# Attention in a four-layer decoder: own values as one rounded product per unit

## The reference, cut to what matters

```
B, S, HID, D, HQ, HK = 64, 32, 512, 128, 32, 8        # cache: 16 pages x 32 keys = 512
q, k, v = x @ Wq.T, x @ Wk.T, x @ Wv.T                # per head of 128
q, k = rope(rmsnorm(q)), rope(rmsnorm(k))
k_all = concat([cache_k (512), k (32)]);  v_all = concat([cache_v (512), v (32)])
scores = q . k_all / sqrt(128), masked where the cache is not valid
o = softmax(scores) @ v_all                           # f32
x = x + o @ Wo.T;  then three more layers of low-rank adapters
```

## Time and profile before

| | |
|---|---|
| runs | 2484.83 us (median of 3, 2483.62 to 2489.36) |
| the profiled execution | 2491.42 us |
| its span, first to last instruction | 2489.6 us |
| TensorE matmuls | busy 2452.9 us, 99% |
| weight loads | 2144.4 us, 86% |
| VectorE | 1591.1 us, 64% |
| ScalarE | 1233.9 us, 50% |
| GpSimd | 768.0 us, 31% |
| mean granted TensorE clock | 0.996 of full |

### The profile page before, as it was taken

One profiled execution on the slowest core, in us unless ns is written; L12 is line 12 of the kernel. 1 busy time (PEld: TensorE's weight loads), 2 busy tenths in 40 slices (PEclk: granted clock), 3 DMA queues, 4 the chain that ended last, 5 costly groups with the idle time before them and its releaser, 6 DMA issues.

```text
span 2489.6 us, 48454 instructions
## 1 busy us (share of the span) xinstructions
PE 2452.9 (99%) x14960; PEld 2144.4 (86%) x14960; DVE 1591.1 (64%) x4346; ACT 1233.9 (50%) x3084; POOL 768.0 (31%) x854
## 2 busy tenths in 40 slices
PE   8999999999999999999999999999999899999998
PEld 6877777778899999999999999999999788888886
DVE  5777777774577777777777777777776434343333
ACT  4677777775455555555555555555555322222221
POOL 5666666665123332222222211112221211110111
PEclk9999999999999999999999999999999999999999
DMA  5233323335898888888888888888887333333331
GB/s 210 72 102 102 99 88 102 95 92 176 309 321 272 283 276 280 274 273 280 273 278 273 283 275 278 277 275 276 277 275 245 103 104 98 107 97 94 103 97 52
DMA packets 390752, 488.57 MB, mean 196 GB/s; under 512 B 53536, under 2 KB 325152, under 8 KB 387616
## 3 DMA queue, kind: packets, MB, share of 16 engines
q1 hardware_dynamic: 353696, 351.89, 45.1%
q0 software_dynamic: 36864, 134.23, 16.4%
HBM read 397.89 MB, written 88.08 MB: 195 GB/s over the span
## 4 chain that ended last, share of the span: by engine, by line
PE 76%; POOL 10%; issue 7%; ACT 4%; DVE 2%; SPq 1%; DMA 0%; POOLq 0%; ACTq 0%; DVEq 0%
PE s_bank L1014 19%; PE o_bank L1028 18%; POOL q_t L498 7%; PE o_bank L1041 5%; PE pt_a L1054 4%; PE pt_b L1054 4%; PE proj L1502 4%; PE proj L1504 4%; PE proj L1503 4%; ACT normed L562 3%; POOL w_hi L458 2%; POOL w_lo L460 1%; PE acc L728 1%; PE acc L729 1%; PE acc L730 1%
## 5 line engine op out<-in xcount | busy, mean ns | idle before, releaser
L929 ACT ACTIVATE probs<-probs,neg_max 128x544 f32<-128x544 f32 x512 | 383.3, 749 | 556.7 <-DVE neg_max L980 556.7
L980 DVE CUSTOM_DVE_ANT_0 probs<-s_bank,mask 128x544 f32<-128x544 f32 x512 | 371.2, 725 | 311.5 <-PE s_bank L1014 246.9
L1028 PEld LDWEIGHTS o_bank<-p_t,v_c 128*128 128x128 f32 x4096 | 537.4, 192 | 26.2
L1014 PE MATMUL s_bank<-k_t,q_t 128*128 128x288 f32 (+1 forms) x2048 | 556.2, 394 | 2.4 <-DVE neg_max L980 2.4
L1028 PE MATMUL o_bank<-p_t,v_c 128*128 128x128 f32 x4096 | 539.6, 275 | 0.0
L1014 PEld LDWEIGHTS s_bank<-k_t,q_t 128*128 128x128 f32 x2048 | 349.8, 191 | 58.5 <-DVE neg_max L980 4.4
L138 POOL DMA_INDIRECT v_c<-in_v_rows,v_row x256 | 249.1, 973 | 299.1 <-PE o_bank L1028 258.2
L728 PE MATMUL acc<-w_hi,x_hi 128*128 128x512 f32 x764 | 314.9, 412 | 0.0
L498 POOL TENSOR_TENSOR q_t<-normed,v_c 128x256 f32<-128x256 f32 x320 | 248.8, 799 | 182.3 <-ACT normed L562 180.4
L729 PE MATMUL acc<-w_lo,x_hi 128*128 128x512 f32 x764 | 301.4, 394 | 0.0
L730 PE MATMUL acc<-w_hi,x_lo 128*128 128x512 f32 x764 | 300.2, 393 | 0.0
(11 more groups left out here) (157 smaller groups left out, 3962.3 us busy)
## 6 DMA issues: line engine op xcount, KB each, us to landing
k_t<-in_k_pages SPq DMA_DIRECT2D x1024, 128.0 KB
q_spill<-wo_early SPq DMA_DIRECT2D x32, 1024.0 KB, 5.3
q_t<-q_spill SPq DMA_DIRECT2D x64, 512.0 KB
o_spill<-o_t SPq DMA_DIRECT2D x64, 512.0 KB
raw<-o_spill SPq DMA_DIRECT2D x64, 512.0 KB, 3.5
k_t<-in_w_qkv SPq DMA_DIRECT2D x11, 1024.0 KB, 8.1
v_spill<-wo_early SPq DMA_DIRECT2D x8, 1024.0 KB, 7.6
k_spill<-wo_early SPq DMA_DIRECT2D x8, 1024.0 KB, 5.2
```

The source lines that it names most:

```text
L929: nc.scalar.activation(probs[:, j % SLOTS_P], probs[:, j % SLOTS_P], ACT.Exp, scale=-1.0, bias=neg_max[:, j % 2:j % 2 + 1], accum_out=row_ ...
L980: nc.vector.tensor_tensor_reduce(out=probs[:, j % SLOTS_P], in0=s_run, in1=mask[:, par], scale=-SCALE, scalar=3.0e38, op0=ALU.add, op1=ALU ...
L1014: last = pe.matmul(s_bank[:, columns].rearrange("p (s t) -> p s t", t=PSIZE), q_t[:, par, g], k_t[:, par, slots, g], start=True, stop=True)
L1028: last = pe.matmul(o_of(n), v_c[:, par, c, g * HD:(g + 1) * HD], p_t[:, i, c], start=n % QUAD == 0 and c == 0, stop=False)
```

## The change

The own values and the own weights are each split into an upper half, rounded to fp32r, and a lower half, the rounded rest. The four 32-row blocks of one 128-row operand then hold for one unit, on the side of the values: upper, upper, lower, zeros; on the side of the weights: upper, lower, upper, zeros. A single fp32r matmul sums upper x upper, upper x lower and lower x upper. It is done for each unit, right after its cache values, in place of four f32 matmuls per quad; and the own weights are transposed for each unit, where they were once per quad.

ScalarE writes the upper values (two copies of 32x1024, once per batch, at unit 5 of the batch before; for batch 0 at unit 2) and evicts the transposed own weights on its own, 128 columns per unit. VectorE writes the lower values (one subtraction of 32x1024, once per batch, behind the work of unit 6, or of unit 2 for batch 0) and one more small subtraction per unit. SP loads the own values as one transfer per batch, one batch further ahead. GpSimd clears only the rows that hold zeros.

```
+    FIRST_VALUES, VALUES_AT = 2, 5
-        v_own = sb("v_own", [P, 2, HK * HD])
+        v_raw = sb("v_raw", [S, 2, HK * HD])
+        v_own = sb("v_own", [P, 2, HK * HD], F32R)
-        own = sb("own", [P, 2, QUAD, S])
+        own = sb("own", [P, SLOTS_P, QUAD, S], F32R)
-        p_t = sb("p_t", [P, 2, KC + 1, ROWS])
+        p_t = sb("p_t", [P, 2, KC, ROWS])
+        own_t = sb("own_t", [P, 2, ROWS], F32R)
...
# SP
             def load_v_own(b, par):
-                at_least(sp, own_summed, (b - 1) * QUADS)
-                for a in range(QUAD):
-                    to = v_own[a * S:(a + 1) * S, par].rearrange("p (q a d) -> p q a d", a=QUAD, d=HD)[:, :, a]
-                    src = v_dram[bass.ds(b * S, S), :].rearrange("s (q a d) -> s q a d", a=QUAD, d=HD)[:, :, a]
-                    sp.dma_start(to, src).then_inc(v_own_in[par], 16)
+                sp.dma_start(v_raw[:, par], v_dram[bass.ds(b * S, S), :]).then_inc(v_raw_in[par], 16)
...
-                    load_v_own(b, par)
-                    if early:
+                    if early and b == 0:
+                        load_v_own(b, par)
+                    if not (early and b == B - 1):
+                        at_least(sp, v_lo_done, b)
+                        load_v_own(b + 1, 1 - par)
+                    if first:
...
-            sp.wait_ge(own_cleared, 2)
+            sp.wait_ge(projected, NSL * NT)
# GpSimd
-            for par in range(2):
-                nc.gpsimd.memset(v_own[:, par], 0.0).then_inc(own_cleared, 1)
+            nc.gpsimd.memset(v_own[3 * S:4 * S, :, :].bitcast(F32), 0.0).then_inc(own_cleared, 1)
+            pool.wait_ge(own_cleared, 1)
+            nc.gpsimd.memset(own[:, :, 3].bitcast(F32), 0.0).then_inc(own_cleared, 1)
# ScalarE, pt_evacuate
-                upto = KC + 1 if is_last(n) else KC
-                if is_last(n):
-                    at_least(act, own_summed, n // QUAD)
-                nc.scalar.activation(p_t[:, i, LOW:upto]..., pt_b[i][:, 0:(upto - LOW) * ROWS],
+                nc.scalar.activation(p_t[:, i, LOW:KC]..., pt_b[i][:, 0:(KC - LOW) * ROWS],
                                      ACT.Copy).then_inc(pt_b_out, 1)
+                at_least(act, own_summed, n - 1)
+                nc.scalar.activation(own_t[:, i], pt_b[i][:, (KC - LOW) * ROWS:(KC - LOW + 1) * ROWS], ACT.Copy)\
+                    .then_inc(own_out, 1)
+
+            def upper_values(b):
+                act.wait_ge(v_raw_in[b % 2], 16 * (b // 2 + 1))
+                at_least(act, own_summed, (b - 1) * HK)
+                if b < 2:
+                    act.wait_ge(projected, NSL * NT)
+                for k in range(2):
+                    nc.scalar.activation(v_own[k * S:(k + 1) * S, b % 2], v_raw[:, b % 2], ACT.Copy).then_inc(v_hi_done, 1)
...
                     n = p * UNITS + j
+                    if n == FIRST_VALUES:
+                        upper_values(0)
+                    if n % HK == VALUES_AT and n // HK + 1 < B:
+                        upper_values(n // HK + 1)
                     if n >= LAG:
                         pt_evacuate(n - LAG, (n - LAG) % 2)
# VectorE
-            def normalise(j):
+            def normalise(n, j):
                 inverse = inv_sum[:, j % 2:j % 2 + 1]
-                nc.vector.tensor_scalar(own[:, j // QUAD % 2, j % QUAD], probs[:, j % SLOTS_P, L:KEYS], inverse, None, ALU.mult)\
+                i, of_own = j % SLOTS_P, probs[:, j % SLOTS_P, L:KEYS]
+                nc.vector.tensor_scalar(own[:, i, 0:3:2], of_own.unsqueeze(1).broadcast_to([P, 2, S]), inverse, None, ALU.mult)\
+                    .then_inc(own_hi_done, 1)
+                nc.vector.tensor_scalar(probs[:, i, 0:L], probs[:, i, 0:L], inverse, None, ALU.mult).then_inc(normed, 1)
+                dve.wait_ge(own_hi_done, n + 1)
+                nc.vector.scalar_tensor_tensor(own[:, i, 1], of_own, inverse, own[:, i, 0].bitcast(F32), ALU.mult, ALU.subtract)\
                     .then_inc(normed, 1)
...
+            def lower_values(b):
+                dve.wait_ge(v_hi_done, 2 * b + 2)
+                nc.vector.tensor_tensor(v_own[2 * S:3 * S, b % 2], v_raw[:, b % 2], v_own[0:S, b % 2].bitcast(F32), ALU.subtract)\
+                    .then_inc(v_lo_done, 1)
...
+                        normalise(n - 1, (j - 1) % UNITS)
+                    if n == FIRST_VALUES:
+                        lower_values(0)
+                    if n % HK == VALUES_AT + 1 and n // HK + 1 < B:
+                        lower_values(n // HK + 1)
# TensorE
+            def weigh_own(n):
+                b, g = n // HK, n % HK
+                if g == 0:
+                    pe.wait_ge(v_hi_done, 2 * b + 2)
+                    pe.wait_ge(v_lo_done, b + 1)
+                pe.wait_ge(own_out, n + 1)
+                pe.matmul(o_of(n), v_own[:, b % 2, g * HD:(g + 1) * HD], own_t[:, n % 2], start=False, stop=is_last(n))\
+                    .then_inc(own_summed, 1)
...
             def turn(n):
+                at_least(pe, own_out, n - 1)
                 if n == 0:
                     pe.wait_ge(copied, NV * NT)
+                    pe.wait_ge(own_cleared, 2)
...
-                if is_last(n):
-                    at = KC - LOW
-                    last = pe.transpose(pt_b[i][:, at * ROWS:(at + 1) * ROWS], own_of(n), ident[:, :])
-                last.then_inc(turned, 1)
+                at = KC - LOW
+                pe.transpose(pt_b[i][:, at * ROWS:(at + 1) * ROWS], own_of(n), ident[:, :]).then_inc(turned, 1)
...
                         weigh_values(n - LAG - 1)
-                        if is_last(n - LAG - 1):
-                            weigh_own((n - LAG - 1) // QUAD)
+                        weigh_own(n - LAG - 1)
```

More of the change, by code:

```diff
@@ L792, in own_of @@
         def own_of(n):
-            return own[:, n // QUAD % 2].rearrange("p u s -> p (u s)")
+            return own[:, n % SLOTS_P].rearrange("p k s -> p (k s)").bitcast(F32)
         def is_last(n):
@@ L801, in attend @@
         load_keys, load_queries, name_values, gather_values = loads
-        v_own_in = [sem("v_own_in0"), sem("v_own_in1")]
+        v_raw_in = [sem("v_raw_in0"), sem("v_raw_in1")]
+        v_hi_done, v_lo_done = sem("v_hi_done"), sem("v_lo_done")
+        own_hi_done, own_out = sem("own_hi_done"), sem("own_weights_out")
         own_cleared = sem("own_cleared")
@@ L843, in emit @@
                     early = isinstance(b, int)
+                    first = early and b < len(WO_WITH)
                     if not (early and b < 2):
@@ L856, in _ @@
                 sp.wait_ge(stored[i], 16 * NSL * (NT // QUARTER) // 2)
-            sp.wait_ge(own_cleared, 2)
+            sp.wait_ge(projected, NSL * NT)
             emit(0)
             emit(1)
-            with sp.Fori(2, PAIRS) as p:
+            with sp.Fori(2, PAIRS - 1) as p:
                 emit(p)
+            emit(PAIRS - 1)
             sp.wait_ge(scored, (B - 1) * HK)
@@ L906, in pt_evacuate @@
                 at_least(act, summed, n - 1)
[L907 to L910 removed]
+                nc.scalar.activation(p_t[:, i, LOW:KC].rearrange("p c n -> p (c n)"), pt_b[i][:, 0:(KC - LOW) * ROWS],
                                      ACT.Copy).then_inc(pt_b_out, 1)
+                at_least(act, own_summed, n - 1)
[8 more added lines that the diff above has]
+                    nc.scalar.activation(v_own[k * S:(k + 1) * S, b % 2], v_raw[:, b % 2], ACT.Copy).then_inc(v_hi_done, 1)
             def o_evacuate(quad):
                 b, q = quad // QUADS, quad % QUADS
[L915 removed]
+                act.wait_ge(own_summed, (quad + 1) * QUAD)
                 if q == 0:
@@ L1033, in o_of @@
                 return o_banks[n // QUAD % 2][:, at:at + ROWS]
-            def weigh_own(quad):
-                par = quad // QUADS % 2
-                if quad % QUADS == 0:
-                    pe.wait_ge(v_own_in[par], 16 * QUAD * (quad // (2 * QUADS) + 1))
-                for n in range(quad * QUAD, quad * QUAD + QUAD):
-                    g = n % HK
-                    last = pe.matmul(o_of(n), v_own[:, par, g * HD:(g + 1) * HD], p_t[:, 1, KC], start=False, stop=is_last(n))
-                last.then_inc(own_summed, 1)
+            def weigh_own(n):
[6 more added lines that the diff above has]
+                    .then_inc(own_summed, 1)
             def turn(n):
@@ L1053, in turn @@
                     bank, at = (pt_a, c) if c < LOW else (pt_b, c - LOW)
-                    last = pe.transpose(bank[i][:, at * ROWS:(at + 1) * ROWS],
-                                        probs[:, n % SLOTS_P, c * P:(c + 1) * P], ident[:, :])
-                if is_last(n):
-                    at = KC - LOW
-                    last = pe.transpose(pt_b[i][:, at * ROWS:(at + 1) * ROWS], own_of(n), ident[:, :])
-                last.then_inc(turned, 1)
+                    pe.transpose(bank[i][:, at * ROWS:(at + 1) * ROWS], probs[:, n % SLOTS_P, c * P:(c + 1) * P], ident[:, :])
+                at = KC - LOW
```

(13 more changed lines are left out.)

9 lines of the change are left out of this document (2 added, 7 removed).

## The result

The changed kernel takes **2520.26 us** (median of four runs, 2519.55 to 2522.99), the kernel before beside it on the same chip 2487.10 (2483.62 to 2491.41). The ratio is 1.0135, with a 95% interval of 1.0115 to 1.0154: slower by 1.4%. The forecast was 2473 with a range of 2452 to 2500, so both its sign and its range were wrong.

A forecast was written before the change was run, and what follows sets the result against it. TensorE's streaming was taken to bound attention. Own block -41, lower-values stall +19 and start +10 sum to -12 us, from the median 2484.83 to about 2473 us; own range 2458 to 2486, wider range with rivals 2452 to 2500.

The forecast's parts named there:

- the own block's gain: TensorE, per quad: four f32 products go, three transposes and four rounded products come; -0.32 us, -41 us over 128 quads.
- the second rival: TensorE's own product: rounded at 128 columns no faster than f32, 0.22 us each; 2536 us in all; chance 0.18.
- the load-bound rival: TensorE's own product: a weight load sets its pace, 0.11 us each; 2493 us in all; chance 0.13.
- The stall: TensorE's score waits once per batch for VectorE's masked maximum of unit 7, behind the lower-values subtraction; 0.30 us, +19 us.
- cheap lower half: VectorE's lower-values subtraction: cheap with 32 partitions or hidden by unseen slack, so no stall; 2454 us; chance 0.12.
- ScalarE is hidden: ScalarE's extra eviction per unit and two copies per batch fit into its waits, with 0.8 us to spare; no cost.
- The start: Batch 0: copies wait for the own values' load, delaying unit 2's exponential and unit 3's maximum; +10 us, between 6 and 12.
- The product, 0.06: TensorE's rounded own product of 128 columns costs 0.06 us; range 0.05 to 0.08.
- a sign of being wrong: Listed under what would show the forecast wrong: transposes starting 0.1 or 0.2 us behind the own product.
- The lower values, 0.30: VectorE's 32x1024 subtraction behind unit 6 delays the next score to 2.72 us in a 2.42 step; 0.30 us in 63 batches.
- The range of the term, 8 to 29: Range in us for all stalls behind the lower-values subtraction, around the forecast +19.
- GpSimd, not in the sum at all: GpSimd (POOL) was only said to clear a smaller part, put at nothing; its overlap with VectorE was forecast at 0.

The follow-up runs named there:

- experiment 1: Changed kernel, but from batch 2 on the lower own values are subtracted for only 32 of 1024 columns (output not the reference's): 2477.56 us, 0.9957 of the kernel before.
- Experiment 5: Kernel before plus one unused 32x1024 VectorE subtraction per batch: behind unit 6 2504.34 us (1.0071), behind unit 4 2532.48 us (1.0182).

## Why the prediction was wrong

**What held.** TensorE sets the time and the own block's gain is real: without the stall a step is 2.444 us, and the product is faster than 0.22 (the second rival), with 0.09 between the forecast's 0.06 and the 0.11 of the load-bound rival. The stall is where it was put, in all batches that split values for the next one, with the masked maximum as its releaser, and it isn't hidden: the "cheap lower half" fell, since 32 partitions took 1.217 us as 128 do (1.224), and experiment 1 gave the stall back. ScalarE is hidden in the steady part. The start is right in its mechanism, the order ScalarE, exponential, VectorE, and near in size:

```profile
643.02 5.95 SPq L834 DMA_DIRECT2D v_raw<-v_spill  x3
...
645.25 2.13 ACT L927 ACTIVATE v_own<-v_raw 32x1024 fp32r<-32x1024 f32 x2 [4.71 <-DMA v_raw<-v_spill]
647.41 0.75 ACT L949 ACTIVATE probs<-probs,neg_max 128x544 f32<-128x544 f32 x1
...
648.66 0.72 DVE L1008 CUSTOM_DVE_ANT_0 probs<-s_bank,mask 128x544 f32<-128x544 f32 x1
```

The exponential of unit 2 stands behind the copies (645.25 to 647.41), and the maximum of unit 3 at 648.66, for 650.5 forecast: SP issued the load at 643.02 rather than 644.8, and ScalarE began 2.2 us later, where 2.6 were taken for the landing. The granted clock was 0.75 from 640 to 646 us, 0.82 to 652 and 0.92 to 660, so it came back more slowly than the 0.72 over 6 us of before, as was forecast.

**The product, 0.06.** It measured 0.09, which with the step 0.027 longer is 512 x 0.027 = 14 us of the gain. The step that failed: the pair's weight load was taken as paced by the transpose load behind it, and that one as "shorter by 0.05, some 0.06" because its record is. The spacing of transposes in the kernel before didn't bear this out:

```profile
1212.93 0.38 PE L1054 MATMUL pt_b<-ident,probs 128*128 128x128 f32 x2
```

The two of `pt_a` at 1212.71 have such loads behind them, and the next pair comes 0.22 later, 0.11 for each. In the changed kernel the next transpose starts 0.15 behind the own product, which the prediction itself had named as a sign of being wrong (0.1 or 0.2). The cost lies between the two terms that it weighed, 0.06 and 0.11. This is a size, not a mechanism. By itself it would have left 2487, still in the range of 2452 to 2500 and near no change.

**The lower values, 0.30.** They measured 0.56. The step of the prediction that failed: "Less 0.09 that two operations overlap, it holds the queue for 1.13", from a place "0.70" in the step. The subtraction took 1218.88 - 1217.63 = 1.25 from start to start, and from the small subtraction (1217.36) to it there are 0.27, where 0.15 was taken from the old scaling pair. It let neither the operation ahead nor the one behind overlap, in any of the kernels here. Why is not shown. It isn't that it has two inputs in SBUF; the large subtraction of the last stage, with two such inputs, is overlapped by the next operation, here in the kernel before:

```profile
1947.75 1.21 DVE L191 TENSOR_TENSOR o_lo<-raw,o_hi 128x1024 fp32r<-128x1024 f32 x1
1948.88 0.22 DVE L1408 TENSOR_SCALAR lang_bias<-expert,lang_f 128x8 f32<-128x8 f32 x1
```

That is 1.13 from start to start, the very number of the prediction. What sets the subtraction of the own values apart is its rows: it reads rows 0 to 31 and writes rows 64 to 95, and its neighbours all begin at row 0. It does so in each kernel here that has it, so no run tells whether that is the cause. The maximum stood 0.22 later than thought, the wait from maximum to score was 0.95 and not 0.89, and with the step 0.02 longer the sum is 0.30 + 0.22 + 0.06 - 0.02 = 0.56. The term is a difference of two near-equal numbers, 2.72 and 2.42; an error of 0.1 in either of its parts is a third of it. The range of the term, 8 to 29, was built from other durations of the subtraction only, and the lost overlap with its neighbours, 0.24, wasn't among them.

**GpSimd, not in the sum at all.** It cost 16 us, more than half of the loss of 29. The step that failed is the assumption that VectorE's durations are constant over the 64 batches. The trace of before showed otherwise, in rows that no group of the front has. VectorE's scalings beside GpSimd's split:

```profile
830.39 0.92 DVE L961 TENSOR_SCALAR probs<-probs,inv_sum 128x512 f32<-128x512 f32 x1
...
831.02 0.76 POOL L883 CAST hi_early<-wo_early 128x512 fp32r<-128x512 f32 x1
...
831.85 1.27 POOL L885 TENSOR_TENSOR lo_early<-wo_early,hi_early 128x512 fp32r<-128x512 f32 x1
...
832.49 0.68 DVE L959 TENSOR_SCALAR own<-probs,inv_sum 128x32 f32<-128x32 f32 x1
```

And by the earlier trace rows's view in two narrower stretches: VectorE's busy time was 230.09 us for 737 instructions from 700 to 1000 and 218.81 for the same 737 from 1600 to 1900. That is 11.3 us for the 13 splits that fall into the first stretch (751 to 991 us), 0.87 each, as the two rows above give (0.92 - 0.48 + 0.68 - 0.24 = 0.88), and it cost nothing while VectorE had slack. The sum asked what VectorE adds, and compared it with the slack of an undisturbed step. Asked for the batch with the least slack, the same working gives 0.87 more there, 20 x 0.87 = 17 us, near the 16 measured. The Trainium skill has the mechanism (SBUF — State Buffer, section "SBUF: two separate sides"): VectorE and GpSimd share a pair of SBUF ports as an exclusive lock held for a whole instruction; on VectorE's side it is taken in the modes that use two ports, and by operations with two SBUF inputs against a GpSimd instruction that reads SBUF. The direction agrees: 0.48 to 0.91, 0.24 to 0.59, and GpSimd's subtraction 1.27 to 2.34 beside VectorE's of 1.22. The sizes agree in part: 1.27 + 1.22 would be 2.49, and the scaling of 842.66 ends at 843.57, within GpSimd's conversion (843.26 to 844.03) and not behind it; the first mask build (634.97 to 636.89) does end behind GpSimd's memset (634.81 to 636.61). No run here separates the lock from another cause of the same overlap.

**What would have shown it.** The answer lay in the step lengths. Before the change the distances from one maximum to the next are 2.22, 2.36, 2.25 and 3.14 in the first quad of a batch; the slack in which once-per-batch work can hide is that of the long step, not the mean of 0.5 per step. Experiment 5 is this argument run: in the old kernel the same operation is free behind unit 6, outside the twenty batches, and costs 0.60 in each batch, some 38 us, behind unit 4. Evening out TensorE's steps is a gain for TensorE and takes away the holes of the others at the same time.

## What to carry to other kernels

Before an operation is put on an engine that releases the bottleneck through a single buffer, write down that engine's slack for each step of the period, in the worst period (with every neighbour that stretches its operations), and put the new operation where the longest step is, or cut it into pieces that each fit. A gain that comes from making the bottleneck's steps equal has to be charged with the work of other engines that the long step used to hide. A stall that is the difference of two near-equal sums deserves a range as wide as the errors of all its parts; the cut into four, the choice of units for the pieces and the later first values were together worth more here (53 us) than the whole shorter step (28); a move by one unit alone was worth nothing, and the cut alone 19.

## What was not expected of the hardware

- A VectorE subtraction of 32x1024 takes 1217 ns, one of 128x1024 1224; one of 32x256 takes 417. Fewer partitions bring nothing, fewer elements in the row do: (1217 - 417) / 768 = 1.04 ns each, and some 0.15 us fixed.
- The subtraction that reads rows 0 to 31 and writes rows 64 to 95 doesn't overlap its neighbours on VectorE: 1.25 us from start to start at a duration of 1.22, where a 128x1024 one of 1.21 is followed after 1.13 and the 128x512 scaling of 0.48 after 0.39. The cause is open.
- A second rounded product of 128 columns costs 0.11 us, what a transpose of 128 columns costs too, and the one in its place 0.09. Its 512-column sibling's 0.24 divided by four isn't its price.
- VectorE and GpSimd beside each other: the scalings 0.48 to 0.91 and 0.24 to 0.59, GpSimd's subtraction 1.27 to 2.34 us, the first mask build 1.06 to 1.92 beside a longer memset, with no wait shown in either engine's rows. The only sign is the longer duration.
